# A recommender's interaction tower on one core: dense numbers transposed and contiguous, quads of four gathered fields, another order at the beginning, the last step by tiles

## The reference, cut to what matters

```python
e = stack([tbl_f[ids[:, f]] for f in range(26)], axis=1)       # 2048 x 26 x 128
combined = concatenate([e, r_dense_x[:, None, :]], axis=1)     # 2048 x 27 x 128
interact = einsum('bfd,bgd->bfg', combined, combined)          # all dot products of the 27 vectors
z = interact[:, TRIU_I, TRIU_J]                                # 351 pairs
h = concatenate([z, r_dense_x], axis=1)                        # 479
h = maximum(h @ W_top1 + b_top1, 0)                            # 512
h = maximum(h @ W_top2 + b_top2, 0)                            # 256
y = h @ W_top3                                                 # 2048 x 1
```

## Time and profile before

| | |
|---|---|
| median of three runs | 396.07 us (392.51 to 396.19) |
| time of the profiled execution | 393.5 us |
| its span, first to last instruction | 391.7 us |
| TensorE matmul busy | 355.5 us (91%) |
| VectorE, ScalarE, GpSimd busy | 187.8, 122.4, 274.1 us |
| granted TensorE clock, mean | 0.996 |
| DMA | 42.21 MB, 108 GB/s over the span |

### The profile page before, as it was taken

The page is one execution under the profiler, slowest core; times in us unless marked ns, Lnnn a source line. Parts: engine busy times, 40 slices in busy tenths (PEclk is TensorE's granted clock), DMA queues, the critical chain, the costliest instruction groups (busy, mean ns, idle before and its releaser), DMA issues.

```text
span 391.7 us, 9605 instructions
## 1 busy us (share of the span) xinstructions
PE 355.5 (91%) x4040; PEld 315.3 (81%) x4040; DVE 187.8 (48%) x392; ACT 122.4 (31%) x232; POOL 274.1 (70%) x263
## 2 busy tenths in 40 slices
PE   0575699999999999999999999999999999968896
PEld 0565689998898988898898978898898978856755
DVE  3876869874156813584256813574256712110100
ACT  1446322223322332323322322332323322341202
POOL 5888888777777777777777777777777777771000
PEclk9989999999999999999999999999999999999999
DMA  7998125343332524243343425243433323242110
GB/s 196 276 276 221 53 59 139 83 117 103 111 103 82 142 58 133 69 122 104 111 101 87 133 71 137 60 121 96 118 95 102 83 73 112 57 129 79 46 51 0
DMA packets 42160, 42.21 MB, mean 108 GB/s; under 512 B 16888, under 2 KB 35920, under 8 KB 42117
## 3 DMA queue, kind: packets, MB, share of 16 engines
q1 hardware_dynamic: 32493, 23.85, 22.0%
q0 software_dynamic: 8192, 16.79, 16.6%
q10 hardware_dynamic: 1431, 0.95, 1.0%
HBM read 32.70 MB, written 8.86 MB: 106 GB/s over the span
## 4 chain that ended last, share of the span: by engine, by line
PE 83%; POOL 6%; DMA 3%; ACT 3%; issue 3%; SPq 1%; DVE 0%; ACTq 0%
PE ps_o L557 36%; PE ps_g L586 14%; PE ps_l L611 9%; PE ps_l L642 7%; PE ps_t L572 7%; PE ps_l L613 7%; POOL rows L228 6%; DMA rows<-tbl,idx 2%; ACT emb L338 2%; DMA idx<-ids_g 1%; DMA turn<-gram 1%; SPq L269 1%; ACT emb L345 1%; PE ps_l L652 1%; PE ps_o L622 1%
## 5 line engine op out<-in xcount | busy, mean ns | idle before, releaser
L228 POOL DMA_INDIRECT rows<-tbl,idx x256 | 273.2, 1067 | 80.3 <-issue 77.4
L487 DVE TENSOR_SCALAR onehot<-ids_b,row_of 128x512 fp32r<-128x512 int16 x320 | 150.2, 509 | 80.6 <-PE ps_o L557 73.9
L557 PE MATMUL ps_o<-onehot,tab 128*128 128x256 f32 (+1 forms) x1280 | 165.7, 287 | 8.3 <-issue 4.6
L557 PEld LDWEIGHTS ps_o<-onehot,tab 128*128 128x128 f32 (+1 forms) x1280 | 158.5, 192 | 9.3 <-issue 5.0
L338 ACT COPY emb<-ps_o 128x512 f32<-128x512 f32 x40 | 31.9, 798 | 124.8 <-PE ps_o L557 124.8
L586 PEld LDWEIGHTS ps_g<-emb 128*54 128x54 f32 x2048 | 53.9, 130 | 15.5 <-issue 6.1
L586 PE MATMUL ps_g<-emb 128*54 128x54 f32 x2048 | 57.7, 214 | 4.9 <-DVE gram L501 1.8
L572 PE MATMUL ps_t<-ident,rows 128*128 128x128 f32 x272 | 42.8, 279 | 16.9 <-DMA rows<-tbl,idx 16.4
L501 DVE COPY gram<-ps_g 128x432 f32<-128x432 f32 x32 | 19.4, 608 | 78.5 <-PE ps_g L586 71.9
L572 PEld LDWEIGHTS ps_t<-ident,rows 128*128 128x128 f32 x272 | 31.9, 142 | 23.9 <-issue 21.1
L345 ACT COPY emb<-ps_t 128x512 f32<-128x512 f32 (+1 forms) x80 | 48.0, 621 | 1.8 <-PE ps_t L572 0.9
(11 more groups left out here) (27 smaller groups left out, 43.8 us busy)
## 6 DMA issues: line engine op xcount, KB each, us to landing
turn<-gram SPq DMA_DIRECT2D x62, 91.1 KB
ids_b<-ids_oh SPq DMA_DIRECT2D x35, 128.0 KB, 3.4
rows<-tbl,idx POOLq DMA_INDIRECT x256, 3.0
turn<-gram SPq DMA_DIRECT2D x62, 43.9 KB
z<-turn SPq DMA_DIRECT2D x64, 40.5 KB
emb<-tbl SPq DMA_DIRECT2D x10, 256.0 KB, 5.6
emb<-tbl SPq DMA_DIRECT2D x10, 192.0 KB
rows<-r_dense_x SPq DMA_DIRECT2D x16, 64.0 KB, 1.9
```

Source lines behind the costliest of these rows:

```text
L228: nc.gpsimd.indirect_dma_start(out=rows[u][:, v, :], out_offset=None, in_=gathered[GATHERED.index(SLOT_OF[v])], in_offset=bass.IndirectOff ...
L487: last = nc.vector.tensor_scalar(onehot[n % BUFS][0:r, i], ids_b[0:r, UNIT * o:UNIT * (o + 1), :], row_of[0:r, k:k + 1], None, ALU.is_equal)
L557: last = nc.tensor.matmul(ps_o[n % 2][:, j, :], tab[0:r, UNIT * o + j, part, k, :], onehot[m % BUFS][0:r, i, j, :], start=(k, j, part) == ...
```

## The change

1. The dense numbers come from the host transposed, per step 128 x 256, with the 256 items in the order of z (tile, item mod 4, group). SyncE loads them once a step into xs[step % 2]; ScalarE copies them into slot 0 of emb (keep_x), and layer 1 reads xs directly, contiguous; its result needs no reordering (by_strip is gone).
2. QUADS are four quads of four gathered slots; rows has 16 slots.
3. Beginning: VectorE makes row_of instead of ScalarE, ScalarE no longer waits for the small weights before its first chunk, the chunks, quads and units are in another order, and VectorE makes 8 one-hots (not 12) before the first chunks, then two one-hots ahead of each later chunk.
4. z is double-buffered by step, so that fetch_z waits for the layer 1 of two steps before. The repeated part of turn is written for the 13 partitions that need it instead of 27.
5. In the last step the layers of step 6 run ahead of the last products, and the last step's own layers run tile by tile (tail_x, tail_z, tail_layer2, tail_layer3), 128 columns wide; y of the two tiles lies on partitions 0 and 64 and is stored separately.

```diff
-QUADS = [range(a, min(NV, a + QF)) for a in range(0, NV, QF)]
+QUADS = [range(a, a + QF) for a in range(1, NV, QF)]
...
 
             p, c = strip_at(s)
             to = turn[u].ap().rearrange("(s i) n -> s i n", s=S4)
             own = gram[p:p + NF, c].rearrange("p j g -> p (j g)")
-            return [(own, to[s, :, 0:NF * GROUPS]), (own[:, 0:LAST_D * GROUPS], to[s, :, NF * GROUPS:])]
-        def z_back(u):
+            wrap = gram[p + WRAP:p + NF, c].rearrange("p j g -> p (j g)")
+            return [(own, to[s, :, 0:NF * GROUPS]), (wrap[:, 0:LAST_D * GROUPS], to[s, WRAP:, NF * GROUPS:])]
...
+            u, e = tile % 2, tile // 2 % 2
+            to = z[e][:, u].rearrange("p s d g -> p s (d g)")
...
+        def tail_chunk(u, n):
+            if u == 0:
+                return ps_o[0][:].rearrange("p a b -> p (a b)")[:, TILE * n:TILE * (n + 1)]
+            return (ps_o[1], ps_t[0])[n // 2][:, n % 2, 0:TILE]
...
-            def load_x(tile):
-                u = tile % 2
-                if tile >= 2:
-                    sp.wait_ge(quad_turned, quad_at(tile - 2, 0) + 1)
-                sp.dma_start(rows[u][:, 0, :], x_t[tile]).then_inc(x_in[u], 16)
+            def load_x(t):
+                if t >= 2:
+                    sp.wait_ge(w1_done, 2 * (t - 1))
+                sp.dma_start(xs[t % 2][:], x[t]).then_inc(x_in[t % 2], 16)
...
-                if t:
-                    sp.wait_ge(w1_done, 2 * t)
+                if t >= 2:
+                    sp.wait_ge(w1_done, 2 * (t - 1))
...
-                sp.dma_start(out.rearrange("b o -> o b")[:, STEP * t:STEP * (t + 1)], y_sb[:]).then_inc(y_out, 16)
+                for u in range(2):
+                    sp.dma_start(out.rearrange("b o -> o b")[:, STEP * t + TILE * u:STEP * t + TILE * (u + 1)],
+                                 y_sb[HALF_P * u:HALF_P * u + 1, :]).then_inc(y_out, 16)
+            def store_tail(u):
+                sp.wait_ge(y_made, STEPS + u)
+                a = STEP * (STEPS - 1) + TILE * u
+                sp.dma_start(out.rearrange("b o -> o b")[:, a:a + TILE], y_sb[HALF_P * u:HALF_P * u + 1, :]).then_inc(y_out, 16)
...
-                if c == 12:
-                    load_x(1)
+            load_x(1)
             load_weights()
-            load_x(2)
...
+            def tail_layer1(u):
+                for half in range(2):
+                    act.wait_ge(w1_tail, 2 * u + (half if u else 1) + 1)
+                    for n in range(2 * half, 2 * half + 2):
+                        nc.scalar.activation(h1[:, n, TILE * u:TILE * (u + 1)], tail_chunk(u, n), ACT.Relu,
+                                             bias=b1_sb[:, n:n + 1]).then_inc(h1_made, 1)
+            def tail_layer2(u):
+                act.wait_ge(w2_done, STEPS + u)
+                act.wait_ge(w3_done, STEPS - 1 + u)
+                for n in range(N2):
+                    last = nc.scalar.activation(h2[:, n, TILE * u:TILE * (u + 1)], ps_l[0][:, n, TILE * u:TILE * (u + 1)],
+                                                ACT.Relu, bias=b2_sb[:, n:n + 1])
+                last.then_inc(h2_made, 1)
+            def keep_x(t):
+                act.wait_ge(x_in[t % 2], 16 * (t // 2 + 1))
+                nc.scalar.copy(x_of(t), xs[t % 2][:].rearrange("p (u s g) -> p u s g", s=S4, g=GROUPS)).then_inc(x_kept, 1)
...
-            act.wait_ge(consts_made, 2)
-            nc.scalar.copy(row_of[:], row_i[:]).then_inc(consts_made, 1)
-            act.wait_ge(small_in, 48)
             def chunks_to(a, b):
                 for c in range(a, b):
                     chunk(c)
 
-            chunks_to(0, 4)
+            chunks_to(0, 6)
+            keep_x(0)
+            chunks_to(6, 10)
+            keep_unit(0, 0)
             keep_quad(0, 0)
-            chunks_to(4, 6)
...
-            chunks_to(6, 8)
+            chunks_to(10, 14)
+            keep_unit(0, 1)
             keep_quad(0, 1)
-            chunks_to(8, 11)
-            keep_unit(0, 1)
+            chunks_to(14, 17)
             keep_quad(0, 2)
-            chunks_to(11, 15)
             keep_unit(0, 2)
+            chunks_to(17, NCHUNKS)
             keep_quad(0, 3)
-            keep_quad(0, 4)
-            chunks_to(15, 19)
+            keep_unit(0, 3)
             keep_quad(1, 0)
-            keep_unit(0, 3)
-            chunks_to(19, NCHUNKS)
             keep_unit(0, 4)
             keep_gram(0)
             keep_quad(1, 1)
             act.wait_ge(chunk_l, NCHUNKS)
             keep_unit(1, 0)
+            keep_unit(1, 1)
             keep_quad(1, 2)
-            keep_unit(1, 1)
+            keep_unit(1, 2)
             keep_quad(1, 3)
-            keep_unit(1, 2)
-            keep_quad(1, 4)
             keep_unit(1, 3)
             keep_unit(1, 4)
...
+            act.wait_ge(small_in, 48)
             for t in range(1, STEPS - 1):
                 a, b = 2 * t, 2 * t + 1
+                keep_x(t)
                 keep_quad(a, 0)
...
+                keep_unit(t + 1, 4)
...
+            keep_x(t)
+            for k in range(NQ):
+                keep_quad(a, k)
             keep_gram(a)
+            layer1(t - 1, 0)
+            layer1(t - 1, 1)
             keep_quad(b, 0)
             keep_quad(b, 1)
-            layer1(t - 1, 0)
+            layer2(t - 1)
             keep_quad(b, 2)
-            layer1(t - 1, 1)
+            tail_layer1(0)
             keep_quad(b, 3)
-            keep_quad(b, 4)
             keep_gram(b)
 
             for h in range(2):
@@ -458,14 +470,13 @@
             for s in range(S4 // 2, S4):
                 for src, to in strip_out(1, s):
                     act.dma_start(to, src).then_inc(turn_out[1], 16)
-            layer2(t - 1)
-            act.wait_ge(w1_done, 2 * t)
+            act.wait_ge(w1_done, 2 * (t - 1))
             act.wait_ge(turn_out[1], TURN_DMAS * 16 * STEPS)
-            for src, to in z_back(1)[DQ:]:
+            for src, to in z_back(TILES - 1)[DQ:]:
                 act.dma_start(to, src).then_inc(z_in[1], 16)
-            for n in range(N1):
-                last_layer1(n)
-            layer2(t)
+            tail_layer2(0)
+            tail_layer1(1)
+            tail_layer2(1)
...
+            dve.wait_ge(consts_made, 2)
+            nc.vector.tensor_copy(row_of[:], row_i[:]).then_inc(row_made, 1)
             for i in range(2):
                 nc.vector.memset(ps_g[i][:], 0.0).then_inc(gram_zeroed, 1)
-            dve.wait_ge(consts_made, 4)
+            dve.wait_ge(row_made, 1)
             per = NCHUNKS // UNITS
             ALL = UNITS * FILLS
-            makes(0, 0, BUFS)
+            makes(0, 0, FILLS)
             for c in range(per):
                 chunk(c)
             for c in range(per, NCHUNKS):
+                n = FILLS // per * c
+                makes(0, n, n + FILLS // per)
                 chunk(c)
-                n = BUFS + FILLS // per * (c - per)
-                makes(0, n, min(ALL, n + FILLS // per))
...
-                if k == 0:
-                    pe.wait_ge(x_in[u], 16 * (tile // 2 + 1))
-                n = sum(1 for v in QUADS[k] if SLOT_OF[v] != F)
-                pe.wait_ge(rows_in[u][k], 16 * n * (tile // 2 + 1))
+                pe.wait_ge(rows_in[u][k], 16 * QF * (tile // 2 + 1))
...
-                    last = nc.tensor.matmul(by_strip(ps_l[bank][:, i, :]), w1_part(2 * bank + i, DB), x_of(t),
+                    last = nc.tensor.matmul(ps_l[bank][:, i, :], w1_part(2 * bank + i, DB), xs[t % 2][:],
                                             start=False, stop=True)
...
+            def tail_x(u):
                 for n in range(N1):
-                    nc.tensor.matmul(by_strip(last_bank(n)), w1_part(n, DB), x_of(t), start=True, stop=False,
-                                     skip_group_check=True)
-                pe.wait_ge(z_in[0], Z_DMAS * 16 * STEPS)
+                    nc.tensor.matmul(tail_chunk(u, n), w1_part(n, DB), xs[(STEPS - 1) % 2][:, TILE * u:TILE * (u + 1)],
+                                     start=n == 0 or (u, n) == (1, 2), stop=False, skip_group_check=True)
+            def tail_z(u):
+                pe.wait_ge(z_in[u], Z_DMAS * 16 * STEPS)
                 for n in range(N1):
                     for blk in range(DB):
-                        nc.tensor.matmul(last_bank(n)[:, 0:TILE], w1_part(n, blk), z_part(blk, 0, 1),
-                                         start=False, stop=False, skip_group_check=True)
-                pe.wait_ge(z_in[1], Z_DMAS * 16 * STEPS)
-                for n in range(N1):
-                    for blk in range(DB):
-                        last = nc.tensor.matmul(last_bank(n)[:, TILE:STEP], w1_part(n, blk), z_part(blk, 1, 2),
+                        last = nc.tensor.matmul(tail_chunk(u, n), w1_part(n, blk), z_part(STEPS - 1, blk, u, u + 1),
                                                 start=False, stop=blk == DB - 1, skip_group_check=True)
-                    last.then_inc(w1_last, 1)
+                    if n % 2:
```

(49 more changed lines are left out.)

110 lines of the change are left out of this document (51 added, 59 removed).

## The result

The changed kernel takes 382.33 us (median of four runs, 379.1 to 384.95), the kernel before 394.69 (four runs beside them, 392.51 to 396.19). The ratio is 0.9664, 95% interval 0.9572 to 0.9756: about 3.4% faster. The profiled execution took 384.95 us with a span of 383.1; it is the slowest of the four, more than 1.5% above the fastest, and the ratio leaves it out.

The account below looks back on a forecast made before the run. TensorE sets the pace, with GpSimd's gathers a second bound just under it. Products 15 at 361.9 plus a 21.0 us tail give span 382.9; 1.8 outside it and half of 2.6 make 386.0 us, range 380 to 391.

Parts of the forecast that it names:

- Dense operand and step: Loop: contiguous dense matmuls save 2.0 us a step, quads 0.1 twice; steps of 41.5 us, 13.4 us over six steps.
- Where it stops: Loop's end: of 18.9 us gained, all but some 5 goes into waiting for tile 14's rows, landing at 337.2.
- rival (c): Whole loop: TensorE's whole gain arrives if gathers end 10 us or more sooner; time 368, chance 0.04.
- Beginning: Start to products of tile 0: 5.5 us gained at the start of the loop, bounds 0 and 9.
- Clock: Waits for tile 14's rows and for z: lower clock costs 2.0 us in front, 1.7 in the tail.
- TensorE's list up to products 15: From tile 14's rows on: TensorE's list, not the last gather, is late; products 15 start at 361.9, 3.8 us sooner.
- Tail: From products 15 to the end: z after 11.7 us, 7.6 behind it, 1.7 for clock; 21.0 against 26.0.
- rival (e): Gather stream: VectorE's dense work starves GpSimd's gathers, stream and end 21 us later, 406; chance 0.08.
- The sum: Whole kernel: 361.9 + 21.0 gives span 382.9; 384.7 with 1.8 outside the span; 386.0 forecast.

Follow-up runs that it names:

- e9: Changed kernel without the gather of the sixteenth field (16 of 256 gathers left out), on a first-kind chip: 383.92 us in one execution, kernel before 395.33.
- e10: Changed kernel with layer 3 of step 6 and the first tile's pair part moved behind the last products: 374.83 us, ratio 0.9527 to the kernel before.
- e11: As e10, with the 12 one-hots before products of tile 0 cut to 8, each paced by TensorE's use: 374.71 us, ratio 0.9549 to the kernel before.
- e12: Changed kernel with the last step as before, 256 columns wide, dense operand contiguous, first-kind chip: 381.2 us, ratio 0.9678 to the kernel before.
- e8: Changed kernel with the old beginning (row_of on ScalarE, wait for small weights, old order), other chip: 510.86 us, ratio 1.0002 to the kernel before.
- e5: Changed kernel with 18 idle matmuls on TensorE in the tail's wait, other chip: 503.38 us, ratio 0.9864 to the kernel before.
- e3: Changed kernel without the gather of the sixteenth field (16 of 256 left out), other chip: 487.63 us, ratio 0.9535 to the kernel before.
- e2: Kernel before without the gather of the sixteenth field, other chip: 487.13 us, ratio 0.9495 to the kernel before.
- e4: Changed kernel with 8 one-hots, not 12, before products of tile 0, each paced by TensorE's use, other chip: 510.58 us, ratio 1.0009 to the kernel before.
- e6: As e5, with 29 more idle matmuls in the waits before tile 14's quads, other chip: 511.02 us, ratio 1.0002 to the kernel before.
- e1: Changed kernel with layer 1's dense operand read out of emb at a stride again, other chip: 518.99 us, ratio 1.0144 to the kernel before.

## Why the prediction was right, and where its steps were not

**Dense operand and step: right.** The steps start at 79.61, 121.03, 162.45 and so on to 328.22, 41.44 us each, 41.5 forecast. The next instruction follows 0.44 us after a dense matmul's start (344.24 to 344.68), 0.433 forecast, 0.93 before. Its row in the page, with the mean of one of its two records (636 ns in the kernel before):

```profile
L636 PE MATMUL ps_l<-xs,w_sb 128*128 128x256 f32 x56 | 16.7, 379 | 0.0
```

**Where it stops: right in size, short of a bound.** The rows of tile 14 landed at 336.43 (337.2 forecast) and its products started at 338.26 (338.4). One sign that I had named failed: TensorE was to wait for rows from about tile 10 on, and it waits for none between the beginning and tile 14, where two of the four quads wait and not each. Wrong is the sentence that TensorE "could come 13 us later and nothing would change". I had looked at who is late for the quad and not at who is late for layer 1 behind it: z of tile 13 arrives some 12 us after the loop's end in e9, at 340.2, only 2.6 us before layer 1 could begin behind the rows. With the loop's end at the forecast 323.3, and not at 328.2, it would have had 5 us more. It changed no number of the sum; but rival (c), 368, can't happen without a quicker z.

**Beginning: wrong, 5.5 us forecast, none in this execution.** Products of tile 0 start at 51.98, at 51.95 before. Bounds 0 to 9 held it at their edge. The timelines of the changed kernel, of PE, then of DVE, then of GpSimd:

```profile
34.92 1.09 PE L595 MATMUL ps_t<-ident,rows 128*128 128x128 f32 x4 [9.60 <-DMA rows<-tbl,idx]
...
51.98 3.52 PE L610 MATMUL ps_g<-emb 128*54 128x54 f32 x128 [0.92 <-issue]
```

```profile
36.90 0.49 DVE L498 TENSOR_SCALAR onehot<-ids_b,row_of 128x512 fp32r<-128x512 int16 x1 [8.64 <-PE ps_o L583]
```

```profile
16.59 2.55 POOL L231 DMA_INDIRECT rows<-tbl,idx  x1 [0.31 <-issue]
19.45 2.56 POOL L231 DMA_INDIRECT rows<-tbl,idx  x1 [0.30 <-issue]
```

The first cast does start sooner, at 7.47 and not 11.93. But the third quad of tile 0 stands ahead of the third unit on TensorE, as it did before, and TensorE now comes to it sooner: it waits 9.60 us for its rows until 34.92, where before it turned that quad at 29.63 without a wait for rows. The unit behind it frees no one-hot buffer, and VectorE idles 8.64 us until 36.90. The rows are late for two reasons that the trace shows. Four gathers took 2.55 us each while VectorE worked without a pause; and after the last of them had ended, at 27.71, the rows took another 7.2 us to land (the median over all gathers is 3.0 from the start), in a stretch in which the DMA engines were full (share 1.02 from 30.0 to 34.9), with tables, weights and lists of ids issued just before. The wait also cost clock: it was at 0.50 from 34.9 to 38.0, and the unit behind took 6.18 us, the next 4.08. I had costed VectorE as the limit: the wait of TensorE's in-order list for the rows of tile 0 was missing from that step.

How long that wait is depends on the execution. e10 has the same beginning instruction by instruction, and there it was 6.0 us (TensorE's waits for rows in e10 in total, their number and the longest; then its products of tile 0):

```profile
PE ps_t L595 <- DMA rows<-tbl,idx: 14.2, 4, 6.0
...
48.09 3.52 PE L610 MATMUL ps_g<-emb 128*54 128x54 f32 x128 [0.92 <-issue]
```

Products of tile 0 start at 48.09 in e10 and 47.74 in e11, at 51.72 in e9 and 51.82 in e12; the loop is left at 324.3 in the first two and at 328.0 to 328.2 in the others and in the changed kernel. So the new beginning yields nothing or about 4 us, and what decides it is open. That the loop is left at 328.2 and not at 323.3 costs nothing, as forecast, since rows and z of the end are later. e8 undoes this part, but on the chip where TensorE is bound otherwise; of the old beginning the first chip has one trace.

**Clock: right, its sizes split otherwise.** Both waits brought it down; a third place, in the beginning, was not in the sum and reached nothing at the end. In front it cost 1.1 in the products and 0.5 in the quad, 1.6 for 2.0 forecast. In the tail: 10.8 us behind z, 8.0 in e10 at a clock of 1.00, so 2.8 for 1.7; e5 on the other chip gives 1.6. The Trainium skill, TensorE: Matmul & The Clock Gate, section HAM oscillation, says that short bursts with transfer waits between them lose the clock each time; both places agree, at 0.50, though the 2.38 us before the second quad of tile 14 alone didn't yet bring it down (1.00 from 330 to 332).

**TensorE's list up to products 15: right.** 360.87 for 361.9. ScalarE's order came as forecast: four activations at 359.13, the copy of the last quad at 360.15, products 0.72 later.

**Tail: its mechanism right, 22.2 for 21.0.** z after 11.46 (11.7 forecast); behind it 8.0 without the clock's loss, in e10, for 7.6; the rest is the clock's. And one question I hadn't asked: whether the order that fills TensorE ahead of products 15 is the good one. It puts 3.5 us of ready work (2.94 of pair matmuls, 0.6 of layer 3) where TensorE is the bound and not into the wait behind, where it has nothing to do, and leaves a wait that costs the clock. Nothing in the sum was wrong by it, but e10 shows about 6 us in that order.

**VectorE against GpSimd, rival (e): seen, and without effect on the stream's end.** The 27th gather ends at 52.06 (51.98 before). The amount of interference stayed the same, as I had counted; its place moved, into the gathers of tile 0 (above). The Trainium skill, SBUF — State Buffer, section SBUF: two separate sides, says that a VectorE operation in a two-port mode locks GpSimd out for as long as that one instruction lasts. The runs bear out less than the reading in (e), by which a whole dense stretch blocks: beside twelve one-hots back to back a gather took 5.42 us, but 3.24 in e10, and one-hots 0.48 us apart leave it at 1.26 or less (e11), which a lock that lasts one instruction doesn't exclude. That these one-hots run in such a mode, no run shows.

**The sum.** Span 383.1 for 382.9. The profiled execution's 384.95 us stands beside the 384.7 of the sum. That it meets so closely is partly luck: 1.0 too late at products 15 against 1.2 too little in the tail. The median 382.33 is 3.7 under the forecast 386.0, most of it outside the sum: half of the distance between profiled execution and median of before that I had added (1.3), and the spread between executions (the other three spans are 377.3, 380.6 and 380.5; that it is the gathers' stream that spreads is my guess from e10 to e12, since these three have no trace). Against those three spans the sum is 2.3 to 5.6 us too long.

**Left open.** Why TensorE stalls for issue on the other chip, and why both e3 and e2, without 16 gathers, lie 22 us under the kernel before there, though hardly anything waits for a gather. The changed kernel itself wasn't run there; that e4, e6 and e8, each a small step from it, tie with the kernel before suggests that its 3.4% is gone there, no more than suggests. The stride (e1), the old beginning (e8) and the idle matmuls (e5, e6) weren't run on the first chip, so that no run there parts the shorter step from the rest of the change. Against the kernel before, e12 has products 15 10.2 us sooner and a tail 2.3 shorter, the changed kernel 4.8 and 3.8.

## What to carry to other kernels

When a second bound lies close under the first, look for the third at once: list for every instruction behind the wait who else would be late for it. In the last stretch, put work that is ready into the wait for the last transfer and not ahead of the instruction that starts it; the same calls in another order were worth about 1.4%, more than the whole rewriting of the tail, and kept the clock up at no cost. At the start, an in-order list fails at the item that waits for another engine's slow stream: when the work ahead of a quad gets shorter, ask when its rows land.

## What the runs showed of the hardware

The same kernel takes 394 us on one chip and 509 on another. In e4 on the second, a near version of the changed kernel, TensorE stops 74 times for 48.5 us in the products and 25 times for 28.5 us in the one-hot matmuls, with no releaser in the trace; the changed kernel on the first chip has 0.9 in its products. A gather beside VectorE's one-hots takes 3.24 to 5.42 us when they come back to back, at most 1.26 when they are paced, 2.55 beside other dense work of VectorE, 0.94 alone. From the end of a gather to its rows it took 7.2 us while the DMA engines were full. A dense matmul's record takes 642 ns with a strided operand and 380 with a contiguous one (e1, e6). Idle matmuls in a wait (36 records, 4.45 us) save 1.6 us of a tail of 18.4. The last gather starts at 353.62, 351.44, 349.81 and 348.88 in four executions of near versions (changed kernel, e12, e10, e11), a spread as large as the smaller effects argued about here.
